# A fused attention and feed-forward kernel: residual added by TensorE in the down product, one gate product per pair of tiles, rounding offset made by two ScalarE passes

## What is computed

```python
def fp4_quant_dequant(x):                       # blocks of 16 along the last dim
    scale = jnp.maximum(jnp.max(jnp.abs(xb), axis=-1, keepdims=True) / 6.0, 1e-12)
    idx = jnp.searchsorted(_MID, jnp.abs(xb / scale))    # grid 0 .5 1 1.5 2 3 4 6
    return _GRID[idx] * jnp.sign(xb / scale) * scale
gate = fp4_linear(x, w_gate)      # fp4_linear quantises both operands
y = fp4_linear(x, w_up)           # x: 4096 tokens x 128, weights 352 x 128
h = jax.nn.silu(gate) * y
return fp4_linear(h, w_down)      # back to 128 channels
```

## Time and profile before

| | us |
|---|---|
| median of 3 runs | 813.99 (813.62 to 816.39) |
| the profiled execution | 816.01 |
| its span | 814.3 |
| busy: PE / DVE / ACT / POOL | 615.5 / 540.7 / 302.3 / 280.1 |

### The profile page before, as it was taken

The page is one execution under the profiler, slowest core; times in us unless marked ns, Lnnn a source line. Parts: engine busy times, 40 slices in busy tenths (PEclk is TensorE's granted clock), DMA queues, the critical chain, the costliest instruction groups (busy, mean ns, idle before and its releaser), DMA issues.

```text
span 814.3 us, 14007 instructions
## 1 busy us (share of the span) xinstructions
PE 615.5 (76%) x5231; PEld 445.5 (55%) x5231; DVE 540.7 (66%) x1126; ACT 302.3 (37%) x555; POOL 280.1 (34%) x328
## 2 busy tenths in 40 slices
PE   2376887888766667679777787798988988676886
PEld 1275875666633334378555565455655655454554
DVE  7615564333249948938889986666667666878784
ACT  2231111333224313412555545344444434455442
POOL 6540000000010000004558777534444445446454
PEclk9565998999989878969899998799999998899898
DMA  8400000000000000000000000000000000000000
GB/s 253 122 1 1 0 1 0 1 1 0 1 1 1 0 1 1 1 1 1 1 0 1 1 2 0 1 2 1 2 2 2 2 2 1 1 14 27 13 27 27
DMA packets 13676, 10.48 MB, mean 13 GB/s; under 512 B 1398, under 2 KB 12598, under 8 KB 13492
## 3 DMA queue, kind: packets, MB, share of 16 engines
q1 hardware_dynamic: 13620, 9.73, 4.2%
HBM read 7.63 MB, written 2.10 MB: 12 GB/s over the span
## 4 chain that ended last, share of the span: by engine, by line
PE 46%; DVE 21%; issue 14%; POOL 11%; ACT 7%; ACTq 0%; DMA 0%; POOLq 0%; DVEq 0%
PE ps L1157 6%; PE ps L1243 5%; PE ps L1374 4%; PE ps L1184 4%; PE ps L1272 3%; POOL G L276 3%; PE ps L1311 3%; DVE r L820 3%; PE ps L1393 2%; PE ps L1290 2%; PE ps L1193 2%; DVE S L828 2%; DVE arena L1017 2%; PE ps L1201 2%; POOL zT L279 1%
## 5 line engine op out<-in xcount | busy, mean ns | idle before, releaser
L1311 PE MATMUL ps<-wdT,xnt 128*128 128x128 f32 (+1 forms) x384 | 58.8, 310 | 45.5 <-ACT xnt L560 45.5
L1311 PEld LDWEIGHTS ps<-wdT,xnt 128*128 128x128 f32 (+1 forms) x384 | 52.5, 216 | 53.7 <-ACT xnt L560 53.3
L276 POOL TENSOR_TENSOR G<-S,hoff 128x704 f32<-128x704 f32 x32 | 48.6, 1518 | 80.5 <-DVE S L931 80.5
L1243 PE MATMUL ps<-G,xw 128*126 128x512 f32 x72 | 47.3, 810 | 30.1 <-ACT xw L505 22.4
L326 POOL TENSOR_TENSOR ln<-mv,lnc 128x4 f32<-128x4 f32 x64 | 13.0, 202 | 153.1 <-DVE mv L700 153.1
L345 POOL MEMSET early<- 128x2560 f32 x2 | 4.5, 2231 | 173.9 <-PE ps L1228 163.6
L553 ACT ACTIVATE xnt<-ps 128x352 f32<-128x352 f32 x64 | 29.7, 463 | 90.9 <-PE ps L1290 90.7
L365 POOL TENSOR_SCALAR_AFFINE_SELECT arena<-arena 128x1024 f32<-128x1024 f32 x32 | 34.9, 1092 | 71.5 <-ACT arena L637 71.5
L1017 DVE TENSOR_TENSOR arena<-ps,tri 128x1024 f32<-128x1024 f32 x32 | 39.2, 1225 | 23.4 <-PE ps L1374 23.4
L1290 PE MATMUL ps<-wguT,xnt 128*128 128x352 f32 x128 | 53.8, 503 | 1.0
L1292 PE MATMUL ps<-wguT,xnt 128*128 128x352 f32 x128 | 51.5, 485 | 3.9 <-DVE S L931 3.9
(11 more groups left out here) (199 smaller groups left out, 1525.0 us busy)
## 6 DMA issues: line engine op xcount, KB each, us to landing
X<-in_x SPq DMA_DIRECT2D x8, 256.0 KB, 4.9
out<-X SPq DMA_DIRECT2D x8, 256.0 KB, 2.3
wqkv<-in_wqkv SPq DMA_DIRECT2D x1, 1024.0 KB
band<-in_band SPq DMA_DIRECT2D x1, 897.8 KB
early<-in_wfc SPq DMA_DIRECT2D x1, 512.0 KB
kI<-in_scaled_eye SPq DMA_DIRECT2D x1, 192.0 KB
wattn<-in_wattn SPq DMA_DIRECT2D x1, 192.0 KB, 6.9
S<-in_wd SPq DMA_DIRECT2D x1, 176.0 KB, 3.6
```

Source lines behind the costliest of these rows:

```text
L276: tt(out=hgrid, in0=hmoved[k], in1=hoff[k][:, :], op=ALU.subtract).then_inc(s["fh_grid"], 1)
L1243: last = mm(ps[0:WI, w, :], xw[:, w * WO:w * WO + WI], G1[:, b, :], start=True, stop=True)
L1311: last = mm(ps[:, T_BANK + 1, k * P:(k + 1) * P], hT[r % 2][0:FK[c], k, c, :], wdT[0:FK[c], c, :], start=(c == 0), stop=(c == 2))
```

## The change

- `residual` is gone from GpSimd (p = 0) and from VectorE (p = 1). `down_mms` ends each tile's group with one more product, the identity times X of that tile, and ScalarE's `down_copy`, now in both phases, writes the sum from PSUM straight into X. The statistics come one step earlier.
- Silu results have four buffers instead of two, and `gated` is one VectorE instruction for a pair.
- The offset is Square with a scale, then, after a wait for that, Identity with a constant bias, both on ScalarE; VectorE's clamp is gone. This applies to x and h, not to the weights' own offset.

```diff
@@ -106,7 +106,7 @@
         XNT = xnt[:, :].rearrange("p (b n) -> p b n", b=B)
         xT = [xnt[:, k * QD * P:(k + 1) * QD * P].rearrange("p (k c) -> p k c", k=QD) for k in range(2)]
         hT = [xnt[:, (8 + 6 * k) * P:(14 + 6 * k) * P].rearrange("p (k c n) -> p k c n", k=2, c=3) for k in range(2)]
-        sil = [xnt[:, 20 * P + k * F:20 * P + (k + 1) * F] for k in range(2)]
+        sil = [xnt[:, 20 * P + k * F:20 * P + (k + 1) * F] for k in range(4)]
         wqkv = sb("wqkv", [P, 2 * H * DH])
         bfc = sb("bfc", [P, P])
         band_store = sb("band", [P, H * WO])
@@ -130,8 +130,6 @@
         zT_store = sb("zT", [P, U * P])
         zT = zT_store[:, :].rearrange("p (u c) -> p u c", u=U)
         hquant = [t[:, 0:2 * F].rearrange("p (k n) -> p k n", k=2) for t in (band_store, zT_store)]
-        down_store = sb("down", [P, 4 * P])
-        down = [down_store[:, 2 * k * P:2 * (k + 1) * P].rearrange("p (k c) -> p k c", k=2) for k in range(2)]
         kI = sb("kI", [P, 3, P])
         g3s = sb("g3s", [P, B, P])
         late = sb("late", [P, 3 * U * P])
@@ -279,11 +277,6 @@
                     tt(out=blocks(hquant[k].rearrange("p k n -> p (k n)")), in0=blocks(hgrid),
                        in1=hblk[k][:, 2, :].unsqueeze(2).broadcast_to([P, 2 * F // BLK, BLK]), op=ALU.mult).then_inc(s["fh_quant"], 1)
 
-                def residual(r):
-                    g.wait_ge(s["f_down_copied"], ffn_pairs(p, r + 1))
-                    tt(out=X[:, 2 * r:2 * r + 2, :], in0=X[:, 2 * r:2 * r + 2, :], in1=down[r % 2],
-                       op=ALU.add).then_inc(s["f_x_done"], 1)
-
                 def step(r):
                     q = (r + FILL) // 2
                     if 0 <= r - 1 < PN:
@@ -292,8 +285,6 @@
                         quantise_x(q)
 
                 def finish(r):
-                    if 0 <= r - 3 < PN:
-                        residual(r - 3)
                     if r >= 6 and r % 2 == 0:
                         layernorm_moments(2, (r - 6) // 2)
                 return step, finish
@@ -549,8 +540,8 @@
                 def silu(t):
                     n = ffn_tiles(p, t)
                     a.wait_ge(s["f_gate"], n + 1)
-                    need(a, "f_h", n - 1)
-                    act(sil[t % 2], ps[:, GATE_BANK, 0:F], ACT.Silu).then_inc(s["f_silu"], 1)
+                    need(a, "f_h", ffn_pairs(p, t // 2 - 1))
+                    act(sil[t % 4], ps[:, GATE_BANK, 0:F], ACT.Silu).then_inc(s["f_silu"], 1)
 
                 def hT_copy(r):
                     n = ffn_pairs(p, r)
@@ -563,20 +554,23 @@
                 def down_copy(r):
                     n = ffn_pairs(p, r)
                     a.wait_ge(s["f_down"], n + 1)
-                    need(a, "f_x_done", n - 1)
-                    act(down[r % 2], ps[:, T_BANK + 1, 0:2 * P].rearrange("p (k c) -> p k c", k=2), ACT.Copy).then_inc(s["f_down_copied"], 1)
+                    act(X[:, 2 * r:2 * r + 2, :], ps[:, T_BANK + 1, 0:2 * P].rearrange("p (k c) -> p k c", k=2), ACT.Copy).then_inc(s["f_x_done"], 1)
 
                 def offset_x(q):
                     n = ffn_quads(p, q)
                     a.wait_ge(s["fx_ratio"], n + 1)
                     need(a, "fx_grid", n)
-                    act(xoff[:, :], ps[:, X_BANK, :], ACT.Abs, scale=RND).then_inc(s["fx_abs"], 1)
+                    act(xoff[:, :], ps[:, X_BANK, :], ACT.Square, scale=SQ).then_inc(s["fx_offset"], 1)
+                    a.wait_ge(s["fx_offset"], 2 * n + 1)
+                    act(xoff[:, :], xoff[:, :], ACT.Identity, bias=lnc[:, 3:4]).then_inc(s["fx_offset"], 1)
 
                 def offset_h(r):
                     n = ffn_pairs(p, r)
                     a.wait_ge(s["fh_ratio"], n + 1)
                     need(a, "fh_grid", n - 1)
-                    act(hoff[r % 2][:, :].rearrange("p (k n) -> p k n", k=2), up_banks(r), ACT.Abs, scale=RND).then_inc(s["fh_abs"], 1)
+                    act(hoff[r % 2][:, :].rearrange("p (k n) -> p k n", k=2), up_banks(r), ACT.Square, scale=SQ).then_inc(s["fh_offset"], 1)
+                    a.wait_ge(s["fh_offset"], 2 * n + 1)
+                    act(hoff[r % 2][:, :], hoff[r % 2][:, :], ACT.Identity, bias=lnc[:, 3:4]).then_inc(s["fh_offset"], 1)
 
                 def step(r):
                     q = (r + FILL) // 2
@@ -584,7 +578,7 @@
                         hT_copy(r - 2)
                     if 0 <= r + 1 < PN:
                         silu(2 * r + 2)
-                    if 0 <= r - 2 < PN and p == 0:
+                    if 0 <= r - 2 < PN:
                         down_copy(r - 2)
                     if r % 2 == 0 and 0 < q <= QN:
                         xT_copy(q - 1)
@@ -893,26 +887,20 @@
                         in1=xblk[:, 1, :].unsqueeze(1).unsqueeze(3).broadcast_to([P, 1, QD * P // BLK, BLK]), op0=ALU.mult,
                         op1=ALU.mult).then_inc(s["fx_ratio"], 1)
 
-                def clamp(name, off, n):
-                    v.wait_ge(s[name + "_abs"], n + 1)
-                    ts(out=off[:, :], in0=off[:, :], scalar1=RND_MIN, scalar2=None, op0=ALU.max).then_inc(s[name + "_offset"], 1)
-
                 def move_x(q):
                     n = ffn_quads(p, q)
-                    clamp("fx", xoff, n)
-                    v.wait_ge(s["fx_offset"], n + 1)
+                    v.wait_ge(s["fx_offset"], 2 * n + 2)
                     need(v, "fx_grid", n)
                     tt(out=xmoved, in0=ps[:, X_BANK, :], in1=xoff[:, :], op=ALU.add).then_inc(s["fx_moved"], 1)
 
-                def gated(t):
-                    n = ffn_tiles(p, t)
-                    v.wait_ge(s["f_silu"], n + 1)
-                    v.wait_ge(s["f_up"], n + 1)
-                    up = up_banks(t // 2)[:, t % 2, :]
-                    tt(out=up, in0=up, in1=sil[t % 2], op=ALU.mult).then_inc(s["f_h"], 1)
+                def gated(r):
+                    v.wait_ge(s["f_silu"], ffn_tiles(p, 2 * r + 2))
+                    v.wait_ge(s["f_up"], ffn_tiles(p, 2 * r + 2))
+                    k = 20 * P + 2 * F * (r % 2)
+                    tt(out=up_banks(r), in0=up_banks(r), in1=pair(xnt[:, k:k + 2 * F]), op=ALU.mult).then_inc(s["f_h"], 1)
 
                 def absmax_h(r):
-                    v.wait_ge(s["f_h"], ffn_tiles(p, 2 * r + 2))
+                    v.wait_ge(s["f_h"], ffn_pairs(p, r + 1))
                     reduce(out=pair(largest_h(r)), in_=blocks(up_banks(r)), axis=AX, op=ALU.max,
                            apply_absolute_value=True).then_inc(s["fh_absmax"], 1)
 
@@ -925,31 +913,22 @@
 
                 def move_h(r):
                     n = ffn_pairs(p, r)
-                    clamp("fh", hoff[r % 2], n)
-                    v.wait_ge(s["fh_offset"], n + 1)
+                    v.wait_ge(s["fh_offset"], 2 * n + 2)
                     need(v, "fh_grid", n - 1)
                     tt(out=pair(hmoved[r % 2]), in0=up_banks(r), in1=pair(hoff[r % 2][:, :]), op=ALU.add).then_inc(s["fh_moved"], 1)
-
-                def residual(r):
-                    v.wait_ge(s["f_down"], ffn_pairs(p, r + 1))
-                    tt(out=X[:, 2 * r:2 * r + 2, :], in0=ps[:, T_BANK + 1, 0:2 * P].rearrange("p (k c) -> p k c", k=2),
-                       in1=X[:, 2 * r:2 * r + 2, :], op=ALU.add).then_inc(s["f_x_done"], 1)
 
                 def step(r):
                     q = (r + FILL) // 2
                     if 0 <= r < PN:
-                        gated(2 * r)
+                        gated(r)
                     if 0 <= r - 1 < PN:
                         move_h(r - 1)
                     if 0 <= r < PN:
-                        gated(2 * r + 1)
                         absmax_h(r)
                     if r % 2 == 0 and q < QN:
                         absmax_x(q)
                     if r % 2 and q < QN:
                         move_x(q)
-                    if p == 1 and 0 <= r - 2 < PN:
-                        residual(r - 2)
                     if 0 <= r < PN:
                         inverse("fh", hblk[r % 2], largest_h(r), ffn_pairs(p, r), ffn_pairs(p, r - 1))
                     if r % 2 == 0 and q < QN:
@@ -958,10 +937,10 @@
                         ratio_h(r)
                     if r % 2 == 0 and q < QN:
                         ratio_x(q)
-                    if p == 0 and 0 <= r - 4 < PN:
-                        v.wait_ge(s["f_x_done"], ffn_pairs(p, r - 3))
-                        tile_stats(2, 2 * r - 8)
-                        tile_stats(2, 2 * r - 7)
+                    if p == 0 and 0 <= r - 3 < PN:
+                        v.wait_ge(s["f_x_done"], ffn_pairs(p, r - 2))
+                        tile_stats(2, 2 * r - 6)
+                        tile_stats(2, 2 * r - 5)
                 return step
             step0, step1 = ffn(0), ffn(1)
 
@@ -1045,7 +1024,7 @@
                     step0(ATT_FILL[n])
             v.wait_ge(s["att_x_done"], TILES)
             tile_stats(1, TILES - 1)
-            for r in range(PN + 4):
+            for r in range(PN + 3):
                 step0(r)
```

(7 more changed lines are left out.)

## The result

The changed kernel takes 877.71 us (median of 4 runs, 876.12 to 879.81) against 814.33 (4 runs, 813.62 to 816.39) for the one before: ratio 1.0775, 95% interval 1.0744 to 1.0806. It is 63 us slower. The forecast was 873, range 846 to 892.

What follows compares the result with a forecast made beforehand. The prediction took the loop through TensorE's and ScalarE's in-order queues as the bound: +40.1 us for the longer loop and +18.6 for clock falls, +58.7 on 816.01, 874.7; less 2.0 for the median, 873 us, range 846 to 892.

Steps and rivals of the forecast that it cites:

- The loop: Feed-forward chain through TensorE's and ScalarE's queues: steps lengthen to 8.48 us even, 8.57 odd, 7.07 late.
- Identity product: Residual on TensorE, ahead of the gate products: two more products per pair, 0.53 us on the loop.
- Second pass: ScalarE's Identity after Square: 0.87 us for h, 0.72 for x; adds 0.91 and 0.76 us to the loop.
- that rival: Square not loaded with Silu on ScalarE: two table loads per step, 82 us more, above 930 us; chance 0.04.
- VectorE sets the end: VectorE's queue sets each step's end, so removing its work makes the kernel faster: 784 us; chance 0.04.
- The clock: TensorE's longer waits before down products lower its clock: 12 falls of 19 at 1.55 us, +18.6 us.
- The rest: Outside steps 2 to 13: first steps +0.45 twice, steps 14 to 18 of p = 0 +3.9, end +1.0 us.
- The lengthened loop: Whole kernel before added clock falls: 20.8 + 13.5 + 0.9 + 3.9 + 1.0 = +40.1 us.

Runs made afterwards that it cites:

- the reordered kernels: TensorE's down product moved behind both tiles' gate and up products, ScalarE's copies behind the first Silu: changed kernel 792.74 us, kernel before 840.3 us.
- the kernel whose clock was held: Changed kernel plus seven unread identity products behind the transposes of h in steps 1 to 11 of both phases: 849.39 us.

## Why the prediction was right

- *The loop.* Right. Steps at the full clock: 8.37, 8.53 and 6.99 us against 8.48, 8.57 and 7.07. Over steps 2 to 13 in the kernel whose clock was held, this makes 98.6 and 97.1 us; the forecast without step 2's low clock was 99.5 and 98.0. That the order of the queues is the cause is shown by the reordered kernels.
- *Identity product.* 0.46 us a pair instead of 0.53, at the full clock. Much of the error in the steps is here.
- *Second pass.* 0.882 us and 0.722 against 0.87 and 0.72; its wait 0.03. The prediction put the passes at 45 us in all; they are 28.2 + 11.6 = 39.8. The changed kernel has the same four table loads as the one before and none between Silu and Square, so that rival is out. The trace agrees with the Trainium skill, ScalarE: Activation LUTs (Table sets), in that Copy needs no load of its own; that Square needs none beside Silu is shown by this trace and is not said there.
- *VectorE.* Off the loop, and clearly idle: it waits 96.9 us ahead of the gate product. The rival "VectorE sets the end" is refuted for the old order. It becomes partly true in the new one, where the paired gate and the missing clamp both shorten odd steps.
- *The clock.* The direction was right, the size low. Seventeen of 19 steps after a wait of 2.9 to 3.2 us ran partly at the 1.2 GHz level, not 12. Changed kernel less clock-held kernel is 16.0 + 14.3 = 30.3 us over steps 2 to 13, where the forecast had 22. Part of the reason is a reading of the rows that was wrong. The prediction has p = 0 wait 2.62 us in every even step; that is step 8 alone, and the other even steps from 4 to 12 waited 2.23 us. So of five waits of 2.5 to 2.6 us three led to a fall, not of nine. The Trainium skill, TensorE: Matmul & The Clock Gate (HAM oscillation), describes waits between bursts that are long enough to make every burst start cold. The prediction left out that condition. In the changed kernel 17 of 19 comes near to every; but in the two kernels with the two passes and without the identity products the same waits of 2.9 to 3.2 us led to 13 and 12 falls of 19, with the paired gate alone five waits of 2.5 us led to none and four of 2.8 us to one, and with the residual alone waits of 2.2 us to three of nine. So the length of the wait alone does not set the number, and what else does is open.

TensorE's wait ahead of the down products of even steps of p = 0, timeline, steps 4, 8 and 10 of the kernel before:

```profile
421.03 1.60 PE L1311 MATMUL ps<-wdT,xnt 128*128 128x128 f32 x12 [2.23 <-ACT xnt L560]
...
448.28 1.60 PE L1311 MATMUL ps<-wdT,xnt 128*128 128x128 f32 x12 [2.62 <-ACT xnt L560]
...
461.71 1.60 PE L1311 MATMUL ps<-wdT,xnt 128*128 128x128 f32 x12 [2.23 <-ACT xnt L560]
```

- *The rest.* First steps, the linear attention's interleaved quad and the end were forecast at +5.8 us and came to +1.7: steps 14 to 16 of p = 0 grew by 2.2 instead of 3.9, the end by 1.4, the stretch between by 0.7, and the program ahead of step 2 of p = 0 was 2.7 shorter. The clock at the start of the two profiles differs (0.74 before and 1.00 after in the first 60 us), but that this makes the 2.7 us was not tested.

The lengthened loop, without any low clock, was forecast at 40.1 - 3.4 = 36.7 us over the kernel before; the kernel whose clock was held is 33.5 us over the kernel before of its group. So the mechanism and the loop were right, and the sizes were not all: two errors of opposite sign (clock 8 us low; products and remainder 6 us high) met in a total 2.4 us low on the profile's own scale. That the total is that close is partly luck.

## What to carry to other kernels

Price added work by its place in an in-order queue, not by that engine's idle time: ask whether the idle time is the other half of a loop through the same queue. When it is, reorder before moving work between engines; here one order made the same instructions 85 us faster. The moved residual (in the second phase) and the second pass (in the first), losses in the old order, were what let the new one win. The longer loop was paid twice here: some 42 us for itself, and some 22 for the clock that TensorE's longer waits brought down.

## What the runs showed of the hardware

**A bf16 clamp on VectorE can be held up by GpSimd.** The same instruction on `xoff` took 0.26 us with GpSimd idle (at 378.38 us in the kernel before), 0.47 in the feed-forward's steps of the kernel before and 1.03 with the paired gate. In the two timelines shown above for step 5 it ends 0.14 to 0.15 us after GpSimd's instruction does (429.05 and 428.90; 426.49 and 426.35), though it began 0.32 us before that end in one and 0.89 us before it in the other. The neighbouring float32 instructions on VectorE keep their 0.69 and 0.89 us. That the clamp waits for GpSimd is read from these times; GpSimd's instruction alone was not taken away.

**Products of no use made a kernel faster.** Four to a step, in waits, took 6 us off the kernel before (0.989, 0.981 to 0.997).
